# Recommender tower on one core: where chunk 1 stops being worked in two half-width parts

## The reference, cut to what matters

```python
e = stack([tbl_f[ids[:, f]] for f in range(40)], axis=1)      # 2048 x 40 x 64
viW = einsum('bpd,pde->bpe', e[:, i_idx], W)                  # 780 pairs, 64x64 each
z   = einsum('bpe,bpe->bp', viW, e[:, j_idx])                 # 2048 x 780
h = concatenate([z, dense_ctx], axis=1)
h = maximum(h @ W_top1 + b_top1, 0)                           # 512
h = maximum(h @ W_top2 + b_top2, 0)                           # 256
y = h @ W_top3
```

## Time and profile before

| | before |
|---|---|
| median of 3 runs | 1567.65 us (1567.61 to 1569.01) |
| the profiled execution's own time | 1575.01 us |
| its span (first to last instruction) | 1572.3 us |
| mean granted TensorE clock | 0.962 |
| busy share PE, DVE, ACT, POOL | 92%, 62%, 55%, 47% |

### The profile page before, as it was taken

One profiled execution on the slowest core, in us unless ns is written; L12 is line 12 of the kernel. 1 busy time (PEld: TensorE's weight loads), 2 busy tenths in 40 slices (PEclk: granted clock), 3 DMA queues, 4 the chain that ended last, 5 costly groups with the idle time before them and its releaser, 6 DMA issues.

```text
span 1572.3 us, 52519 instructions
## 1 busy us (share of the span) xinstructions
PE 1453.6 (92%) x21300; PEld 651.2 (41%) x21300; DVE 972.5 (62%) x841; ACT 870.1 (55%) x6611; POOL 741.2 (47%) x891
## 2 busy tenths in 40 slices
PE   4788989879889999989999999999999999999999
PEld 2344645535455433333333443333443443333333
DVE  2554545536555545566777665677777655679990
ACT  0544344436546644456867573455767643458992
POOL 6434434454444433436666564446676644553220
PEclk7788999989999999999999999999999999999999
DMA  4232223223222112222222222222222212222200
GB/s 124 64 106 68 77 63 80 70 57 84 72 76 73 49 48 52 76 60 51 58 60 65 50 52 59 70 70 59 57 60 59 57 54 59 73 60 60 57 9 14
DMA packets 60957, 98.79 MB, mean 63 GB/s; under 512 B 17062, under 2 KB 17078, under 8 KB 60715
## 3 DMA queue, kind: packets, MB, share of 16 engines
q1 hardware_dynamic: 35876, 65.08, 14.2%
q0 software_dynamic: 20224, 20.75, 7.1%
q10 hardware_dynamic: 4614, 9.61, 1.9%
HBM read 95.37 MB, written 0.01 MB: 61 GB/s over the span
## 4 chain that ended last, share of the span: by engine, by line
PE 88%; issue 6%; another core or an unknown queue 3%; DVE 3%; ACTq 0%; ACT 0%; DVEq 0%
PE u L1182 37%; PE u L1168 22%; PE zacc L1196 18%; PE u L1238 5%; PE u L1111 2%; DVE prod L1066 2%; PE u L1255 2%; PE u L1226 1%; PE u L1214 0%; DVE row_prod L1035 0%; DVE row_prod_v L1035 0%; DVE row_sums L1076 0%; ACTq L754 0%; ACT L880 0%
## 5 line engine op out<-in xcount | busy, mean ns | idle before, releaser
L926 ACT ACTIVATE row_prod<-row_prod 128x64 f32<-128x64 f32 x3248 | 777.0, 241 | 191.4 <-DVE row_prod L1035 146.6
L1066 DVE TENSOR_TENSOR prod<-u,emb 128x1024 f32<-128x1024 f32 x496 | 593.3, 1218 | 348.3 <-remote 151.0
L1182 PE MATMUL u<-emb,weights 64*32 64x512 f32 (+1 forms) x9760 | 753.0, 520 | 50.4 <-issue 32.7
L812 POOL DMA_INDIRECT gathered<-tbl,index x512 | 487.3, 952 | 568.5 <-DVE prod L1066 240.5
L926 ACT ACTIVATION_READ_ACCUMULATOR row_prod<-row_prod 128x1 f32 x3248 | 609.7, 188 | 3.9 <-issue 3.9
L1168 PE MATMUL u<-row_weights,emb 64*32 64x512 f32 (+5 forms) x5632 | 467.0, 534 | 22.3 <-issue 15.1
L1182 PEld LDWEIGHTS u<-emb,weights 64*32 64x32 f32 x9760 | 277.9, 108 | 382.6 <-issue 268.6
L1196 PE MATMUL zacc<-prod,band 64*32 64x512 f32 (+1 forms) x4960 | 403.9, 515 | 16.9 <-issue 12.4
L1035 DVE TENSOR_TENSOR row_prod<-u,first_fields 128x1024 f32<-128x1024 f32 x203 | 247.1, 1217 | 138.9 <-PE u L1168 83.3
L1168 PEld LDWEIGHTS u<-row_weights,emb 64*32 64x32 f32 x5632 | 150.6, 108 | 218.7 <-issue 137.7
L1196 PEld LDWEIGHTS zacc<-prod,band 64*32 64x32 f32 x4960 | 159.0, 109 | 167.2 <-issue 153.0
(11 more groups left out here) (41 smaller groups left out, 228.1 us busy)
## 6 DMA issues: line engine op xcount, KB each, us to landing
weights<-w_pairs SPq DMA_DIRECT2D x155, 256.0 KB
row_weights<-w_rows SPq DMA_DIRECT2D x90, 256.0 KB
gathered<-tbl,index POOLq DMA_INDIRECT x512
w12s<-w_top ACTq DMA_DIRECT2D x8, 832.0 KB
w12s<-w_top ACTq DMA_DIRECT2D x4, 512.0 KB
first_fields<-tbl,index POOLq DMA_INDIRECT x120
h<-tbl SPq DMA_DIRECT2D x2, 224.0 KB
h<-tbl ACTq DMA_DIRECT2D x2, 224.0 KB
```

The source lines that it names most:

```text
L812: pool.indirect_dma_start(out=to, out_offset=None, in_=tables[2 * t + e], in_offset=bass.IndirectOffsetOnAxis(ap=index[:, col:col + 1].bit ...
L926: last = nc.scalar.activation(x, x, ACT.Copy, accum_out=row_sums[:, c % 2, s, q:q + 1])
L1066: nc.vector.tensor_tensor(result, products, x, ALU.mult).then_inc(prod_ready, 1)
L1182: last = nc.tensor.matmul(u[of, b, h, to], weights[half, x % WRING, unit, of], y, start=True, stop=True)
```

## The change

Only chunk 0 is ordered anew. It now has three parts: samples 0 to 255 with the tiles 0 to 15 and the column steps 0 to 63 (steps 0 to 59: 32 `two` and 28 row steps), the same for samples 256 to 511 (steps 60 to 119), and the rest for all 512 samples at once (steps 120 to 195: 60 column steps of full width and the 16 row steps of tiles 16 to 19). The second part is written in the order in which its tiles arrive, like the first. `PART_STEPS` gives its gathers the steps 30 + 1.8 per field, and the rest's 88 + 4 per field. Other changes follow from it: weights are loaded for the new parts, sums are batched by part, and `copied_before` and `last_copy` name the waits on copies of `zacc`.

```diff
-FIRST_PART = 44
-FIRST_STEPS = 2
+PART_STEPS = {1: (30, 1.8), 2: (88, 4)}
 CHUNK_STEPS = {1: (115, 3.9), 2: (277, 4.9), 3: (477, 4.9)}
...
 PARTS = 2
+PART_TILES, PART_COLUMNS = 16, 64
...
     for q in range(PARTS):
-        twos = [("two", *COLUMN_STEPS[m:m + 2], q) for m in range(0, N_COLUMNS, 2)]
-        rows = [("row", x[1], q * SUB // PARTS + x[2] // PARTS) for x in ROW_STEPS if x[2] % PARTS == 0]
+        twos = [("two", *COLUMN_STEPS[m:m + 2], q) for m in range(0, PART_COLUMNS, 2)]
+        rows = [("row", x[1], q * SUB // PARTS + x[2] // PARTS) for x in ROW_STEPS
+                if x[2] % PARTS == 0 and max(tiles_used(x)) < PART_TILES]
         mixed = []
-        if q == 0:
-            for t in [*range(1, SINGLE[0], 2), *SINGLE]:
+        if q < PARTS:
+            for t in [*range(1, SINGLE[0], 2), *SINGLE] if q == 0 else range(1, PART_TILES, 2):
                 now = [x for x in rows if max(tiles_used(x)) <= t]
                 ready = [x for x in twos if max(tiles_used(x)) <= t]
                 rows, twos = rows[len(now):], twos[len(ready):]
                 mixed += spread(ready, now)
         steps += mixed + spread(twos, rows)
-    return steps
+        bounds.append(len(steps))
+    rest = [x for x in ROW_STEPS if max(tiles_used(x)) >= PART_TILES]
+    waiting, mixed = COLUMN_STEPS[PART_COLUMNS:], []
+    early = [x for x in waiting if max(tiles_used(x)) < PART_TILES]
+    mixed += early
+    waiting = waiting[len(early):]
+    for t in range(PART_TILES, T):
+        now = [x for x in rest if max(tiles_used(x)) == t]
+        ready = [x for x in waiting if max(tiles_used(x)) <= t]
+        waiting = waiting[len(ready):]
+        mixed += spread(ready, now)
+    assert not waiting
+    return steps + mixed, bounds
...
 def parts(c):
-    return range(PARTS) if c == 0 else range(1)
+    return range(PARTS + 1) if c == 0 else range(1)
+
+
+def halved_part(c, q):
+    return c == 0 and q < PARTS
...
-    begin, every = CHUNK_STEPS[c] if c else (FIRST_PART, FIRST_STEPS)
-    steady = begin + every * f
+    begin, every = CHUNK_STEPS[c] if c else PART_STEPS[q]
+    steady = begin + every * (f - 2 * part_tiles(c, q)[0])
```

More of the change, by code:

```diff
@@ L181 @@
 PARTS = 2
+PART_TILES, PART_COLUMNS = 16, 64
+assert all(max(tiles_used(x)) < PART_TILES for x in COLUMN_STEPS[:PART_COLUMNS])
 def make_whole():
@@ L318, in make_loads @@
 def make_loads():
-    out = [(SLOT_DONE.get(x - WRING, -1), 2 * x / WRING, "slot", x) for x in range(STREAMS * WSLOTS)]
+    out = [(SLOT_DONE.get(x - WRING, -1), 2 * x / WRING, "slot", x) for x in range(len(GIVEN_SLOTS))]
     out += [(PIECE_DONE.get(x - PIECE_RING, -1), 2 * x / PIECE_RING - 1, "piece", x) for x in range(len(PIECES))]
@@ L363, in make_batches @@
     for c in range(CHUNKS):
-        width = len(parts(c))
         batches = []
         for q in parts(c):
+            width = PARTS if halved_part(c, q) else 1
+            here = part_columns(c, q)
             for g in range(GROUPS):
-                end = Z_FIRST[g + 1] if g < LAST_GROUP else N_COLUMNS
-                for m in range(Z_FIRST[g], end, SUMB * width):
+                begin = max(Z_FIRST[g], here.start)
+                end = min(Z_FIRST[g + 1] if g < LAST_GROUP else N_COLUMNS, here.stop)
+                for m in range(begin, end, SUMB * width):
                     batches.append((q, g, range(m, min(m + SUMB * width, end))))
@@ L376, with product_of @@
 SUMS_BEFORE = [sum(len(BATCHES[x]) for x in range(c)) for c in range(CHUNKS)]
+def product_of(c, q, m):
+    if halved_part(c, q):
+        x, half = divmod(m, PARTS)
+        return q * PART_COLUMNS // PARTS + x, half
+    return m, 0
 def last_product(c, j):
     q, _, columns = BATCHES[c][j]
-    return (q * N_COLUMNS + columns[-1]) // len(parts(c))
+    return product_of(c, q, columns[-1])[0]
 PRODUCT_SUMMED = {}
@@ L394, with copied_before, last_copy @@
 for c in range(CHUNKS):
-    for j, (q, g, _) in enumerate(BATCHES[c]):
-        Z_GROUPS[c, g, q] = j
+    for j, (q, g, columns) in enumerate(BATCHES[c]):
+        if columns[-1] + 1 in (*Z_FIRST, N_COLUMNS):
+            Z_GROUPS[c, g, q] = j
 Z_ORDER = list(Z_GROUPS)
+def copied_before(c, j):
+    done = [x for x in Z_ORDER if (x[0], Z_GROUPS[x]) < (c, j)]
+    return done[-1] if done else None
+def last_copy(c, g):
+    return max(x for x in Z_ORDER if x[:2] == (c, g))
 TOPS = [(1, 0), (1, 2), (2, 0), (3, 0)]
@@ L458, in issue_step @@
     here = NEEDS[c, q, i]
-    before = NEEDS[c, q, i - 1] if i else here - 4
+    before = NEEDS.get((c, q, i - 1), here - 4)
     in_time = c * N + before + j * (here - before) / 4 - 14
-    begin, every = CHUNK_STEPS[c] if c else (FIRST_PART, FIRST_STEPS)
-    steady = begin + every * f
+    begin, every = CHUNK_STEPS[c] if c else PART_STEPS[q]
+    steady = begin + every * (f - 2 * part_tiles(c, q)[0])
     return max(1, int(min(in_time, steady)))
@@ L475, in make_transposes @@
         for q in parts(c):
-            new, t = [], 0
-            while t < T:
+            new, t = [], part_tiles(c, q)[0]
+            while t in part_tiles(c, q):
                 new.append((c, t, q))
@@ L489, in turned @@
 def turned(c, step, q):
-    return max(TURN_OF[c, t, q] for t in tiles_used(step))
+    return max(TURN_OF[c, t, turned_in(c, t, q)] for t in tiles_used(step))
 def make_transpose_steps():
@@ L531, in make_reducers @@
     rows = [c * N + n for c in range(CHUNKS) for n in ROWS[c]]
-    early = [x for x in rows if x < N // PARTS and max(tiles_used(FIRST[x])) <= EARLY]
+    early = [x for x in rows if x < PART_ENDS[0] and max(tiles_used(FIRST[x])) <= EARLY]
     on_vector = set(early[EARLY_EVERY - 1::EARLY_EVERY])
@@ L550, in make_gathers @@
         for q in parts(c):
-            for t in range(T):
+            for t in part_tiles(c, q):
                 if (c, q) == (0, 0) and t in MADE:
@@ L1026, in multiply @@
                             dve.wait_ge(rows_reduced, r - ROW_RING + 1)
-                    if n == min(x for x in ROWS[c] if part_of(c, x) == q):
+                    if n == min(x for x in ROWS[c] if part_of(c, x) == q) and 0 in part_tiles(c, q):
                         for t in range(FT):
@@ L1175, in pair_step @@
                     unit = (column_of(c, n) + i) % SLOT
-                    to = samples(c, i) if step[0] == "two" else slice(0, CB)
+                    to = samples(0, i) if step[0] == "two" else slice(0, CB)
                     for h, g in itertools.product((0, 1), range(TILES)):
@@ L1197, in sum_step @@
                                                 band[half, TILE - 1 - r:2 * TILE - 1 - r],
-                                                prod[half, (c * N_COLUMNS + x) % PRING, h, samples(c, i)],
+                                                prod[half, (c * N_COLUMNS + x) % PRING, h, samples(0, i) if halved_part(c, q) else slice(0, CB)],
                                                 start=(r == 0), stop=Z_LAST[g, bank, cg] == (m, h, e))
```

52 lines of the change are left out of this document (33 added, 19 removed).

## The result

| | before | after |
|---|---|---|
| median of 4 runs each, us | 1568.33 (1567.61 to 1571.01) | 1555.13 (1554.11 to 1556.79) |
| ratio, 95% interval | | 0.9891 (0.9866 to 0.9917) |
| the profiled execution's own time | 1575.01 | 1554.11 |
| its span | 1572.3 | 1552.3 |

The change makes the kernel 13 us faster. The time lies inside the range of the prediction, 25 us above its 1530, with a bit over a third of the 37 us.

The account below looks back on a forecast made before the run. TensorE was taken as bound, getting instructions slowly while POOL makes gathers. Chunk 0 summed to 188 + 139 + 149 = 476 us against 513, 37 less: 1538 from the profiled 1575.0, 1530 after 7.4 us down to the median; range 1507 to 1556.

Parts of the forecast that it names:

- A: Steps 0 to 59 of chunk 0, forecast to end at 188 us, range 184 to 192, with 88 gathers.
- B: Steps 60 to 119 of chunk 0, forecast 139 us: array 65.4 plus 70 gathers at 1.05; ends 118 and 143.
- C: Steps 120 to 195 of chunk 0, forecast 149 us: array 91.2 plus 78 gathers at 0.745.
- the array's 91.2: TensorE's own need in steps 120 to 195: 60 column steps at 1.29 us and 16 row steps at 0.86.
- loss per gather: A stretch's time beyond the array's need, divided by its gathers: 1.11 us in part 1 before, 0.90 and 0.59 at full width.
- Rival 1: Blind to width: each gather costs TensorE 1.11 us however wide the matmuls; total 1563, chance 0.07, cut in half.
- rival 2: Pure instruction rate: TensorE begins 32.0 records a us wherever gathers run; total 1472, chance 0.07.
- 7 are held by the ring until step 60's transposes: Gathers of part 1's tiles 8 and 9, asked for by step 59, were to run only after step 60 began.
- It is a tie, and costs nothing: Steps from 60: ScalarE's ten rows, 27 to 30 us, against TensorE's 30; uncovered by gathers, up to 15 us.
- Edits with no price: 19 fewer weight loads, one fewer `zacc` copy, two fewer transpose groups, new rings' waits: nothing counted for them.
- Rival 3: Slower: gathers in bursts make TensorE crawl through steps 60 to 195, 1.39 us per gather; total 1605, chance 0.06.
- The rule: From the Trainium skill: crossing an instruction block is mostly hidden, so fewer instructions would buy nothing; total 1563.

Follow-up runs that it names:

- the pair without gathers of the second group: Changed kernel and kernel before, each without the 480 gathers of chunks 1 to 3: 1161.65 us (1.0198 of before) and 1137.73 us (0.9994).
- narrow_rest: Changed kernel with each full-width column matmul of steps 120 to 195 in chunk 0 cut into two of half the columns: 1570.23 us, 0.9998 of before.
- paced: Changed kernel with part 1's gathers of tiles 8 and later at later, closer steps, and chunk 1's gathers starting later: 1549.87 us, 0.9880 of before.
- even_order: Changed kernel with part 1's row steps spread evenly among its column steps instead of in order of the tiles' arrival: 1546.63 us, 0.9849 of before.
- relief_2: Changed kernel with every second of part 1's first fifteen row steps reduced by VectorE instead of ScalarE: 1550.69 us, 0.9878 of before.
- narrow_end: Changed kernel with column matmuls cut into two of half the columns in chunk 3's last 84 steps: 1559.15 us, 0.9931 of before.
- plain_before: Kernel before with every indexed gather made a plain transfer of 128 following table rows, same queue and bytes: 1131.98 us, 0.7198 of before.
- plain_gather: Changed kernel with every indexed gather made a plain transfer of 128 following table rows, same queue, bytes and place: 1156.60 us, 0.7471 of before.

## Why the prediction was right in sign and too high in gain

Both pairs together, each stretch with indexed gathers, with plain ones, and what lies between, per gather:

| us | A | B | C | sum |
|---|---|---|---|---|
| before: indexed, plain | 148.0, 83.2 | 140.7, 82.2 | 182.8, 98.4 | 471.5, 263.8 |
| lost to gathers | 64.8 / 64 = 1.01 | 58.5 / 61 = 0.96 | 84.4 / 88 = 0.96 | 207.7 |
| after: indexed, plain | 162.1, 86.8 | 133.8, 99.5 | 158.5, 98.2 | 454.4, 284.5 |
| lost to gathers | 75.3 / 72 = 1.05 | 34.3 / 56 = 0.61 | 60.3 / 85 = 0.71 | 169.9 |

The change takes 37.8 us out of what indexed gathers cost. That this is near the forecast's 37 is luck: 24.2 of it sit in B, where no matmul got wider, and the forecast's came for the most part from C. And it adds 20.7 us of its own, 17.3 of them in B and 14.7 of those in the steps 60 to 79 (42.4 us for 27.7). The forecast put nothing there. The plain rows are from two groups; the pair without gathers of the second group, one chip, gives the same stretches as 89.3, 81.3 and 98.5 us before and 94.0, 99.5 and 98.2 after, 22.6 more, and the steps 60 to 79 again as 42.4 for 27.7. (As said, A, B and C together are compared; the parts are to see where it sits. That steps 60 to 79 are ScalarE's shows by themselves: it is busy 40.71 of the 42.40 us, and row_prod has 81.9% of the chain of waits there.) The two numbers aren't quite independent: where TensorE waits for ScalarE anyway, a gather costs it nothing, which is part of B's low 0.61. So the 37.8 must not be read as the gain by width. Point by point:

- *What bounds it: gathers slow TensorE's instructions.* Right, and shown: with the same transfers made without an index, both kernels lose a quarter or more of their time. C takes 98.2 us with plain transfers, 7 above the array's 91.2, which is then part of every loss per gather here. (The 98.4 us of the kernel before are for 48 half-width column steps and 28 row steps, 86.0 us of array, with ScalarE busy 95.2 of them: the two don't compare the widths.)
- *C, loss per gather at full width 0.745.* Right: (158.5 - 91.2) / 85 = 0.79. The forecast had 78 gathers there and 85 came, chunk 1's among them, since POOL ran behind its steps. At half width in the column matmuls alone, narrow_rest, it loses (172.9 - 91.2) / 83 = 0.98 per gather; with the sums narrow too that would be about 1.05 (an estimate, by the share of the records), near part 1's 1.11. So the worth of the width, 29 us in the forecast (178 - 149), was high by about 8 and not the step that failed. Rival 1 falls with this (0.9998 where it is made true), and rival 2 with 1796 + 1788 records in 158.5 us, 22.6 per us and not 32.0.
- *A, 184 to 192.* Wrong by 16 us, the largest single miss: the step "7 are held by the ring until step 60's transposes". They were, but TensorE makes those transposes ahead of step 60's multiplication, so all 7 ran in 190 to 200 us, before step 60. A had 72 gathers instead of 64. At B's own 1.05 that is 8.4 of the 16; the rest lies in steps 50 to 59, 33.2 us with 16 gathers for 19.5 with 10. The 8.4 don't count in the sum, since B then had 56 gathers and not 70. In paced, A is 144.5 us with 64 gathers, as forecast (146), and B takes back all of it.
- *B, "It is a tie, and costs nothing".* This is the step that failed: a term put at nothing that had a cost. By its own numbers B with 56 gathers is 65.4 + 56 x 1.05 = 124.2; it took 133.8, 9.6 more. Where the run is broken up the sum holds: even_order's B is 123.3 us with 55 gathers (123.2 by the sum), relief_2's 127.2 with 56. Where A's miss is repaired and the run left, it doesn't: paced's B is 146.9 with 64 gathers (132.6 by the sum). The bound named with it, "without that cover up to 15 us", is met where gathers cost nothing (14.7). With indexed gathers part of it is covered, but not all: taking half the rows from ScalarE gained 6.0 us in steps 60 to 79. What makes the other 3 or 4 us of the 9.6 isn't shown.
- *Edits with no price, chunk 1 unchanged.* Right: chunk 1 takes 375.8 us (376 forecast, 378.4 before). MATMUL records fell from 21300 to 19860, the 1440 forecast. Rival 3, crawls all through, didn't come: C's clock is 0.98. One crawl is left where chunk 1's gathers begin (31 records in 340 to 350 us), as there was one before.
- *The median.* I took 7.4 us off the sum since the profiled execution before lay that far above its median. The changed kernel's lies 1 us below its own. So 20.9 us between the profiled executions are 13.2 between the medians: 8 of the 25 us of miss are this term. The other 17 are chunk 0, which ends 20 us later than forecast, less 3 us that came behind it. Most of the 20 are B's 9.6 and the 7.6 of A that no shifted gather explains.
- *The rule.* That fewer instructions would buy nothing is refuted: narrow_rest's are dearer by 14.0 us beside gathers, and narrow_end's by 5.1 without any. But this isn't shown to be a matter of fetching instructions. The Trainium skill (Runtime: NRT & Kernel Launch, section Instruction fetch mechanics) says only that what crossing a block costs is mostly hidden, and the traces don't speak against that. The pages of the kernel before and of plain_before have the larger instruction queue as

```profile
q8 instruction: 167, 2.74, 0.7%
```

```profile
q8 instruction: 167, 2.74, 1.0%
```

in packets, MB and share of the DMA engines' time: of 1572 and of 1131 us, 11 us both times, so these packets took no longer beside indexed gathers. And in 340 to 355 us, where TensorE began 59 records, the profile has no instruction packet under way.

What stays open: what in an indexed gather holds TensorE's instructions back (plain_gather changes the instruction on POOL, its time and which rows of the table are read, all at once), why in one group of runs nothing did, and how much of the 3.6 us that A costs with plain transfers is the order and how much the gathers' steps.

## What to carry to other kernels

A run of one kind of step at one engine that comes out as a tie isn't to be priced at nothing: here it cost 6 to 10 us of the 15 that it costs uncovered. The order that follows the arrival of data isn't free for the engine that takes that kind of step. When two kernels are cut at the same step numbers, count what work lies in each stretch before reading a gain off it; and when an experiment takes back a part of an edit, scale its result by that part. And before tuning around indexed gathers, measure the kernel once with plain transfers in their place, as a measure of what they cost: here some 400 us, thirty times the change.

## What the runs showed of the hardware

It isn't the number, the size or the queue of a gather's transfers that costs TensorE its pace. The kernel before moves 60957 packets and plain_before 60956, over the same queue (whether it matters that an indexed gather reads scattered rows, no run tells). In 340 to 355 us, with 10 indexed gathers, the kernel before began 59 records of TensorE, and one step, 124, began on VectorE. In plain_before the steps 120 to 131, with 21 transfers, chunk 1's first among them:

```profile
186.20:201.20 15.00, 14.78 (x443) 8.68 (x428) 14.14 (x14) 15.00 (x125) 11.13 (x21) 1.00 0.55 158
```

871 records, 12 steps instead of one, and the granted clock at 1.00 instead of 0.60. The changed kernel crawls too where chunk 1's gathers begin, at a granted clock of 0.97:

```profile
340.00:350.00 10.00, 7.64 (x31) 1.24 (x30) 0.24 (x2) 0.00 (x0) 6.17 (x7) 0.97 0.11 25
```

So a low clock isn't what starves TensorE there, and I read it at step 60 and at 340 us as what a starved TensorE gets. And the same program took 1138.6 us in one group of runs and 1546 to 1574 in the others, a difference as large as that between plain and indexed gathers; there the indexed gathers took POOL as long, and TensorE didn't wait for them.
